# Attention stage of a fused Trainium2 kernel: a third buffer of probabilities, two operations moved from DVE to POOL, and both weight pieces of a turn split by ACT and DVE

## What is computed

```python
Wqk = jnp.einsum('hij,hkj->hik', tril, tril)
xh = x.reshape(bs, seq_len, H, d)                     # 16, 113, 16, 16
t = jnp.einsum('bshd,hde->bshe', xh, Wqk)
scores = jnp.einsum('bshe,bthe->bhst', t, xh) / jnp.sqrt(d)
attn = jax.nn.softmax(scores, axis=-1)
Vh = (x @ Wv.T + bv).reshape(bs, seq_len, H, d)
out = jnp.einsum('bhst,bthd->bshd', attn, Vh).reshape(bs, seq_len, emb_dim)
return out @ Wo.T + bo
```

## Time and profile before

| | |
|---|---|
| time, median of 3 runs | 1436.33 us (1435.38 to 1437.99) |
| the profiled execution: its time | 1424.37 us |
| its span in the profile | 1422.2 us |
| busy over the span: PE, DVE, ACT, POOL | 73%, 73%, 53%, 40% |
| mean granted clock of TensorE | 0.858 |
| attention stage, first to last step of a turn | about 1045 to 1208.6 us |

### The profile page before, as it was taken

How to read it: one execution, slowest core, us unless ns; L and a number is a source line. 1 busy time by engine, 2 the same in 40 slices (tenths; PEclk the granted TensorE clock), 3 DMA queues, 4 the chain that set the end, 5 groups by cost and what they waited for, 6 DMA issues and landing times. The chain is left out here.

```text
span 1422.2 us, 28260 instructions
## 1 busy us (share of the span) xinstructions
PE 1034.2 (73%) x9099; PEld 698.1 (49%) x9099; DVE 1031.1 (73%) x2238; ACT 751.4 (53%) x1493; POOL 564.6 (40%) x674
## 2 busy tenths in 40 slices
PE   3548778763399997685756869266479997459996
PEld 2422223223265663463544766144456665448885
DVE  5779999987455655647977865788758886746665
ACT  5557777742375663215435654243348887334442
POOL 0248888862244434721001100000026665335663
PEclk9669999995699999886968979688769999579998
DMA  6001111101265654312000000000023332322231
GB/s 235 16 6 54 38 44 45 37 1 53 82 162 151 171 143 155 91 34 89 1 1 1 1 1 1 1 0 0 0 77 103 109 121 76 105 50 77 78 78 36
DMA packets 50611, 89.66 MB, mean 63 GB/s; under 512 B 10740, under 2 KB 34111, under 8 KB 49635
## 3 DMA queue, kind: packets, MB, share of 16 engines
q1 hardware_dynamic: 41840, 64.19, 14.3%
q0 software_dynamic: 8352, 21.67, 5.9%
q10 hardware_dynamic: 288, 2.10, 0.5%
HBM read 73.04 MB, written 16.05 MB: 63 GB/s over the span
## 5 line engine op out<-in xcount | busy, mean ns | idle before, releaser
L1133 POOL TENSOR_TENSOR scan_ch<-scan_hs,scan_ct 128x452 f32<-128x452 f32 x128 | 143.6, 1144 | 41.1 <-DVE scan_hs L1247 41.0
L1158 PE MATMUL scan_py<-scan_ch,ident 128*128 128x452 f32 x256 | 131.4, 604 | 37.2 <-POOL scan_ch L1133 27.8
L1247 DVE TENSOR_TENSOR_SCAN scan_hs<-scan_abar,scan_bx 128x452 f32<-128x452 f32 x128 | 133.0, 1080 | 1.4 <-DVE scan_bx L1239 0.8
L1158 PEld LDWEIGHTS scan_py<-scan_ch,ident 128*128 128x128 f32 x256 | 41.7, 196 | 105.6 <-POOL scan_ch L1133 98.2
L2275 DVE TENSOR_SCALAR m3x_a<-m3x_ph,m3x_b 128x128 f32<-128x128 f32 x184 | 49.7, 343 | 58.4 <-ACT m3x_ah L2253 58.4
L1207 ACT ACTIVATE scan_abar<-ssm_dt,ssm_a 128x448 f32<-128x448 f32 x128 | 80.0, 634 | 13.8 <-DVE scan_hs L1247 13.2
L2253 ACT ACTIVATE m3x_ah<-m3x_ph,m3x_b 128x128 f16<-128x128 f32 x184 | 49.9, 383 | 70.4 <-PE m3x_ph L463 39.9
L3204 POOL TENSOR_TENSOR mha_prob_lo<-mha_prob,mha_prob_hi 113x452 f16<-113x452 f32 x64 | 65.8, 1051 | 37.7 <-ACT mha_prob_hi L3373 37.7
L461 PE MATMUL m3x_ph<-m3x_xb,m_w_hi 128*128 128x128 f16 x368 | 74.0, 220 | 2.5 <-DVE m3x_al L2286 1.8
L462 PE MATMUL m3x_ph<-m3x_xb,m_w_hi 128*128 128x128 f16 x368 | 74.0, 220 | 0.0
L463 PE MATMUL m3x_ph<-m3x_xb,m_w_lo 128*128 128x128 f16 x368 | 73.8, 220 | 0.0
(11 more groups left out here) (702 smaller groups left out, 3835.7 us busy)
## 6 DMA issues: line engine op xcount, KB each, us to landing
mha_wbuf<-m3w SPq DMA_DIRECT2D x32, 512.0 KB, 3.3
scan_piece<-m0w SPq DMA_DIRECT2D x30, 256.0 KB, 2.7
m0x_b<-m0b SPq DMA_DIRECT2D x57, 128.0 KB, 3.4
m_out<-m0x_yo SPq DMA_DIRECT2D x57, 128.0 KB, 2.3
tok_wbuf<-m0w SPq DMA_DIRECT2D x5, 768.0 KB, 12.0
m3x_b<-m3b SPq DMA_DIRECT2D x23, 128.0 KB
m_rows<-m0r_parts SPq DMA_DIRECT2D x4, 448.0 KB
m_res<-h SPq DMA_DIRECT2D x1, 1792.0 KB, 8.1
```

The costliest lines, as they stand in the source:

```text
L1133: pool.tensor_tensor(ch[r][:], hs[r][:], ct[n % 2][:], ALU.mult).then_inc(weighed, 1)
L1158: pe.matmul(py[c][:, 0:GT], core.ident[:], ch[u % R][:], start=n == 0, stop=n == NS - 1).then_inc(summed, 1)
L1247: dve.tensor_tensor_scan(hs[u % R][:], abar[c][:, 0:GT], bx[u % R][:], 0.0, ALU.mult, ALU.add).then_inc(scanned, 1)
```

## The change

- `exponential` and `round_prob` use three buffers of probabilities, numbered (j * 4 + g) % 3, and the wait is for one group fewer: `p_low` at j * 4 + (g - 2).
- `repeat_peaks` and `split_o` are done by POOL, in its queue between low parts 0, 1 and low parts 2, 3.
- `scale` and `low_scaled` are gone. DVE does `low` for both pieces of a turn, both at the head of its turn, in one instruction each from the unscaled piece.
- TensorE's `weigh_v(j, 3)` moves into turn j+1, behind `second_pass(j+1, 0)` and `first_pass(j+2, 0)`.
- ACT's `exponential(j, 2)` moves ahead of `take_q(j+2)`.
- `rec` is gone: the reciprocal is written into `o`, and the product replaces it there; the reciprocal now has the wait for `ol_ready` that the product had.

```diff
-    def scale(self, act, n):
-        act.wait_ge(self.hi_done, n + 1)
-        act.activation(self.buf[n % self.depth][:], self.buf[n % self.depth][:], ACT.Copy, scale=WS).then_inc(self.scaled, 1)
-
     def low(self, dve, n):
         dve.wait_ge(self.hi_done, n + 1)
         dve.scalar_tensor_tensor(self.place(n, self.w1l, self.w2l), self.buf[n % self.depth][:], WS,
                                  self.place(n, self.w1h, self.w2h), ALU.mult,
                                  ALU.subtract).then_inc(self.lo_done[n % self.depth], 1)
-
-    def low_scaled(self, pool, n, before):
-        pool.wait_ge(self.scaled, before + 1)
-        pool.tensor_tensor(self.place(n, self.w1l, self.w2l), self.buf[n % self.depth][:],
-                           self.place(n, self.w1h, self.w2h), ALU.subtract).then_inc(self.lo_done[n % self.depth], 1)
...
-        prob = [st.sb(f"prob{r}", [L, HG, L]) for r in two]
+        prob = [st.sb(f"prob{r}", [L, HG, L]) for r in range(3)]
...
+                def repeat_peaks(j):
+                    pool.wait_ge(maxed, j * 4 + 4)
+                    need(pool, mt_ready, j)
+                    pool.tensor_scalar(peaks8[:], peak[j % 2][:].unsqueeze(1).to_broadcast([L, 8, H]), -1.0 / MS, None,
+                                       ALU.mult).then_inc(peaks_ready, 1)
+
+                def split_o(j):
+                    pool.wait_ge(oh_ready, j + 1)
+                    need(pool, out_ready, j)
+                    pool.tensor_tensor(ot_lo[:], o[:], ot_hi[:], ALU.subtract).then_inc(ol_ready, 1)
...
+                repeat_peaks(0)
                 for j in range(NB):
-                    for g in range(4):
-                        pool.wait_ge(p_high, j * 4 + (g + 1))
-                        pool.tensor_tensor(prob_lo[g][:], prob[g % 2][:], prob_hi[g][:],
-                                           ALU.subtract).then_inc(p_low, 1)
-                    mw.low_scaled(pool, 2 * j + 1, j)
+                    low_prob(j, 0)
+                    low_prob(j, 1)
+                    if j + 1 < NB:
+                        repeat_peaks(j + 1)
+                    if j > 0:
+                        split_o(j - 1)
+                    low_prob(j, 2)
+                    low_prob(j, 3)
+                split_o(NB - 1)
...
                     if ahead1:
                         first_pass(j + 1, 1 - p, 0)
+                    if behind:
+                        weigh_v(j - 1, 1 - p, 3)
...
                         weigh_v(j, p, 2)
-                        weigh_v(j, p, 3)
...
-                    need(act, p_low, j * 4 + (g - 1))
-                    act.activation(prob[g % 2][:], heads(s2[g % 2]), ACT.Exp, scale=0.25).then_inc(exped, 1)
+                    need(act, p_low, j * 4 + (g - 2))
+                    act.activation(prob[(j * 4 + g) % 3][:], heads(s2[g % 2]), ACT.Exp, scale=0.25).then_inc(exped, 1)
...
+                    if now:
+                        exponential(j, 2)
                     if ahead2:
                         take_q(j + 2)
                     if now:
-                        exponential(j, 2)
                         exponential(j, 3)
...
                         mw.high(act, 2 * j)
                         mw.high(act, 2 * j + 1)
-                        mw.scale(act, 2 * j + 1)
...
                 def normalize(j):
                     dve.wait_ge(pv_done, j * 4 + 4)
-                    need(dve, o_made, j)
-                    dve.reciprocal(rec[:], pacc[:, KC * L:2 * KC * L]).then_inc(rec_ready, 1)
+
+                    need(dve, ol_ready, j)
+                    dve.reciprocal(o[:], pacc[:, KC * L:2 * KC * L]).then_inc(rec_ready, 1)
                     dve.wait_ge(rec_ready, j + 1)
...
+                    dve.tensor_tensor(o[:], pacc[:, 0:KC * L], o[:], ALU.mult).then_inc(o_made, 1)
...
                     if behind:
                         mw.low(dve, 2 * j - 2)
+                        mw.low(dve, 2 * j - 1)
...
                         maxima(j + 1, 1 - p, 3)
-                        repeat_peaks(j + 1, 1 - p)
-                    if behind:
-                        split_o(j - 1)
-                    if ahead1:
                         split_peaks(j + 1, 1 - p)
```

More of the change, by code:

```diff
@@ L1499, in __init__ @@
         self.landed, self.lo_done = ([st.sem(f"w_{n}{p}") for p in range(depth)] for n in ("landed", "lo"))
-        self.hi_done, self.scaled = st.sem("w_hi"), st.sem("w_scaled")
+        self.hi_done = st.sem("w_hi")
         self.small, self.ready = st.sem("small_landed"), st.sem("mult_ready")
@@ L3160, in stage_attention @@
         am = [st.sb(f"am{p}", [128, L], F16) for p in two]
-        prob = [st.sb(f"prob{r}", [L, HG, L]) for r in two]
+        prob = [st.sb(f"prob{r}", [L, HG, L]) for r in range(3)]
         prob_hi, prob_lo = ([st.sb(f"{n}{g}", [L, HG, L], F16) for g in range(4)] for n in ("prob_hi", "prob_lo"))
-        rec, o = st.sb("rec", [128, KC * L]), st.sb("o", [128, KC * L])
+        o = st.sb("o", [128, KC * L])
         ot_hi, ot_lo = (st.sb(n, [128, KC * L], F16) for n in ("ot_hi", "ot_lo"))
@@ L3199, in _, with low_prob @@
                 pool.memset(unit[:, :, 0:HD], 1.0).then_inc(ones_set, 1)
-                for j in range(NB):
-                    for g in range(4):
-                        pool.wait_ge(p_high, j * 4 + (g + 1))
-                        pool.tensor_tensor(prob_lo[g][:], prob[g % 2][:], prob_hi[g][:],
-                                           ALU.subtract).then_inc(p_low, 1)
-                    mw.low_scaled(pool, 2 * j + 1, j)
+                def repeat_peaks(j):
[7 more added lines that the diff above has]
+                    pool.tensor_tensor(ot_lo[:], o[:], ot_hi[:], ALU.subtract).then_inc(ol_ready, 1)
+                def low_prob(j, g):
+                    pool.wait_ge(p_high, j * 4 + (g + 1))
+                    pool.tensor_tensor(prob_lo[g][:], prob[(j * 4 + g) % 3][:], prob_hi[g][:],
+                                       ALU.subtract).then_inc(p_low, 1)
+                repeat_peaks(0)
+                for j in range(NB):
+                    low_prob(j, 0)
[7 more added lines that the diff above has]
+                split_o(NB - 1)
             @block.tensor
@@ L3372, in round_prob @@
                     need(act, pv_done, j * 4 + (g - 3))
-                    act.activation(prob_hi[g][:], prob[g % 2][:], ACT.Copy).then_inc(p_high, 1)
+                    act.activation(prob_hi[g][:], prob[(j * 4 + g) % 3][:], ACT.Copy).then_inc(p_high, 1)
                 def take_o(j):
@@ L3436, in maxima @@
                                       axis=AX.X).then_inc(maxed, 1)
[L3438 to L3442, removed]
                 def split_peaks(j, p):
@@ L3474, in prologue @@
                         maxima(0, 0, g)
-                    repeat_peaks(0, 0)
                     split_peaks(0, 0)
```

## The result

| | before | changed |
|---|---|---|
| median of 12 runs each | 1435.14 us (1431.63 to 1442.83) | 1449.46 us (1440.51 to 1454.76) |
| changed / before | | 1.0098, 95% interval 1.0077 to 1.0118 |
| span of the profiled execution | 1422.2 us | 1447.0 us |
| mean granted clock | 0.858 | 0.852 |

The changed kernel is 14 us slower (1.0098 x 1435.14 - 1435.14), inside the range and near the 1448.0 of the forecast. The spans differ by 24.8, more than the medians: 12.6 of it lies ahead of the attention stage (the first `split_peaks` starts at 1044.61 before and at 1057.17 after), in code that the change does not touch. The profiled execution of before was faster than any of its 12 timed runs. From that first `split_peaks` to the start of the last `add` the stage takes 163.62 us before and 1232.55 - 1057.17 = 175.38 after: 11.8 more.

What follows compares the result with a forecast made beforehand. A 9.47 us ACT-POOL loop bounds each turn; the change opens it, leaving the DVE loop at 9.23 + 1.14 = 10.37. 13 turns x 0.90 = +11.7 on the median 1436.33 gives 1448.0 us, range 1442.5 to 1459.5.

Steps and rivals of the forecast that it cites:

- The loop that was to rule: DVE's queue to normalize's product, TensorE to the transposition, ACT's take_qm, DVE again: 10.37 us a turn after the change.
- A: The forecast case: the DVE loop rules, +0.90 us a turn, +7.8 to +16 in all; chance 0.60.
- Step (1): Scaling on ACT (1.06) and low_scaled on POOL (2.13) go, opening the first loop; three probability buffers open it again.
- the first loop: ACT's scaling, POOL's low_scaled and low probabilities, ACT's last exponential, to the next scaling: 9.47 us, today's turn.
- Step (2): repeat_peaks and split_o (0.23, 0.40) leave DVE's idle gap for POOL (0.45, 0.62): 0 on the turn.
- Step (3): low(2j-1) added at the head of DVE's turn: 1.14 us, in full on the second loop.
- the second loop: The loop through DVE, normalize's product, TensorE and ACT's take_qm: 9.23 us in the kernel before, 0.24 under the ruling one.
- Step (4): weigh_v(j, 3) on TensorE moves into the next turn; covered, as are the rec merge and earlier third exponential: 0.
- The ends of the stage: Turns 0 and 1: 0, give or take 1; last two turns: 0, give or take 1.5.
- Rival B: POOL's queue overlaps DVE's next weight piece: 0.25 to 0.4 a turn more, +15 to +17 in all, 1452; chance 0.12.
- Rival C: TensorE's longer wait before weigh_v 0 drops the clock: 0.85 x up to 12, +22 in all, 1458; chance 0.20.

Runs made afterwards that it cites:

- the cut piece: The changed kernel with DVE's second low part of a turn cut to 8 of its 1024 columns: 1426.71 us, ratio 0.9927.
- the weight part: Run without it: the changed kernel with ACT's scale and POOL's low_scaled back and one low on DVE: 1435.06 us, ratio 1.0002.
- the first experiment: The changed kernel with repeat_peaks and split_o back on DVE: 1481.48 us in one run, beside 1433.57 for the kernel before.
- the fourth: The changed kernel with low(2j-1) moved on DVE from the head of the turn to between the last maximum and split_peaks: 1451.18 us, ratio 1.0111.

## Why the prediction was right, and where it was not

The direction, the mechanism and the place were right. The loop that was to rule does: the bare wait of TensorE for `mha_o`, DVE idle only before `split_peaks`, and no wait of ACT for POOL are all in the profile after, and the cut piece shows the loop to the hundredth. The near hit of the total, 1448.0 against 1449.46, is luck in part: the turns gave 8.2 of the 11.7, and the clock, which the forecast left to a rival, some 5. Nor do the turns speak for the lower end of A (+7.8): the transposition did come 7.58 after 0, close to the 7.55 given there, but TensorE's own work sets that time, and POOL's peaks are done 0.23 ahead of it.

- **Step (1), the first loop.** Removing `scale` and `low_scaled` opened it. That three buffers open it "a second time" was wrong: without the weight part the turn stays at 9.47, since the same POOL chain also ends in `weigh_v` 1. In the sum it cost nothing, since the weight part was there.
- **Step (2), 0 for the two moved operations.** Failed as a statement about the changed kernel. Counted against the kernel before, the gap hid them; but the gap is a gap only while POOL pauses too. In the new rhythm they would have met POOL's low parts and grown from 0.63 to 2.23 us. Their price on POOL (0.53 and 0.61, against 0.45 and 0.62) was right within 0.08, and so was the cover of the peaks; for `split_o` TensorE waits 0.21 each turn, off the loop.
- **Step (3), the price of 1.14.** Right: 1.06 for 1016 of the 1024 columns, with 0.08 left for the small instruction that stays.
- **The terms of the loop.** 10.37 was 0.27 too long. The queue up to the product is 5.27 (1141.06 to 1146.33), not 4.28 + 1.14 = 5.42: in the turn of before `split_v` had started 0.13 late, behind ACT's `take_v`, a wait too short for the view to name. From `weigh_v` 0 to the transposition it is 1.77, not 1.89: the wait for POOL inside that stretch was 0.20 and not 0.08. Both are small waits that I had taken for work. Without them the loop gives 10.10, and the second loop of the kernel before was 8.96 rather than 9.23.
- **Step (4).** Off the loop, as said; its worth for the clock, some 10 us, was not seen.
- **The ends of the stage.** Turns 0 and 1: -2.3 where 0 was said, turn 14 and the last two +6.0 where 0.9 was: the clock on both sides, at another place in each execution.
- **Rival B**, POOL in DVE's way at the head of the turn: not seen; the pair of pieces lasts 2.35 as two free ones would. But POOL's last low part ends at 1151.12 and DVE's next piece starts at 1151.16: 0.04 apart, not 0.25. What the rival rests on did show, in the gap: in the first experiment DVE's peaks and `split_o` end only after POOL's low parts, and in the fourth POOL's peaks after DVE's piece. The Trainium skill (SBUF — State Buffer, section "SBUF: two separate sides") has whichever starts first hold the ports for its whole instruction; the runs agree, with 0.76 and 0.84 lost by DVE and 0.90 by POOL. The peaks on DVE have only one input in the data memory, so the rule as the prediction gave it, for two inputs, would have left them out; that they are held up is the trace's word. In all three the loss is the overlap less about 0.14 (0.89, 0.99 and 1.05 of overlap), and so it is in the row that the prediction weighed the rule against (0.52 of overlap, 0.38 lost): that row was a full block too. Had I asked of each step in DVE's gap what POOL does at that time, (2) would have had its price.
- **Rival C**, the clock: its condition came true in part. The changed kernel's wait is 0.85 and two of 0.20, not 1.5 in one piece, and the clock fell once in the profiled execution. Its price was put at 0.85 a turn for the stretch on the loop; a cold turn in fact costs 3.8 (13.91 less 10.10), and TensorE as a whole is then the limit: in the changed kernel it is busy all of the 20 us from 1200 to 1220, at 0.50.

## What to carry to other kernels

Idle time of an engine ahead of a wait is free only for work that holds up no other engine and is held up by none: before an operation of DVE or POOL is moved into or out of such a gap, or the gap itself moves, look at what the other of the two runs there in the new rhythm, not in the old one. Where several loops lie within a few per cent (here 9.47, 8.96 and TensorE's own 8.8), compute each from work alone, and take out the small waits inside it by comparing the same stretch in a turn where it is not held up. And once TensorE waits in every turn, how the waits are spread can matter as much as the turn's length.

## What the runs showed of the hardware

- POOL and DVE shut each other out until the other's instruction was done: DVE's `tensor_scalar` of 128 columns took 0.99 in place of 0.23 and its two-operand subtraction 1.24 in place of 0.40 beside POOL's low parts; POOL's `tensor_scalar` took 1.43 in place of 0.53 beside DVE's weight piece. What was lost was the overlap less about 0.14 each time. DVE's maxima, which read TensorE's accumulators, kept their 1.16 to 1.17 a pair beside POOL's low parts (1143.33 in the changed kernel).
- With the turn at 10.10 in all three, the clock fell once in the changed kernel (waits of 0.85, 0.20, 0.20), never in turns 2 to 14 with the first wait filled down to 0.20, and every third turn with 0.57, 0.20 and 0.43. A fall cost 3.8 us where the clock rose again some 10 us later (0.50 from 1104.5 to 1114.6 in that kernel), and 5.7 in the changed kernel, where it stayed down past 1220. Each of these is one profiled execution. What decides it beyond that is open.
